# First down projection: each weight block loaded once, the weight sums made on VectorE and moved, the product without token sums put second

## The chip, the cores and the metric

One core of a Trainium2 chip. The time is device microseconds of the core for one execution of the whole program; lower is better. TensorE does the matmuls; VectorE, ScalarE and GpSimd compute beside it; SyncE issues most DMAs (on the hardware queue q1), GpSimd issues those that add to what already lies in the destination (on the software queue q0).

## What is computed

Two feed-forward blocks one after the other on 1024 tokens of width 512. The first ("conditioning") has 1376 hidden features and a low-rank addition of rank 16 per batch entry in each of its three projections; the second has 1792 hidden features and a normalisation before it. All in float32.

```python
def lora_add(base, inp, A, B):
    t = einsum('bri,bni->bnr', A[0][lora_indices], inp)
    return base + einsum('bor,bnr->bno', B[0][lora_indices], t) * 0.5
gate = lora_add(x @ W_gate.T, x, A_gate, B_gate)
up   = lora_add(x @ W_up.T,   x, A_up,   B_up)
act  = silu(gate) * up
down = lora_add(act @ W_down.T, act, A_down, B_down)      # the first down projection
nx   = down * rsqrt(mean(down**2) + 1e-5) * ln_w
out  = x + (silu(nx @ gate_w.T) * (nx @ up_w.T)) @ down_w.T
```

## The kernel before

**Exactness.** Every operand of a matmul is split in two parts of the fast float type: a high part, copied by ScalarE (`hi_...`), and a low part, the raw value minus the high part, from VectorE (`lo_...`). A product is three matmuls (high by high, low by high, high by low).

**Strassen's form.** Each big product is cut in 2x2 blocks and computed as seven products of sums of blocks instead of eight. For that, sums of weight blocks and sums of activation blocks ("token sums", over the two halves of the tokens and of the features) are made first.

**Order of the work.** (1) The first feature tiles; (2) eight groups (`group(j)`, j = 0 to 7, so S1 = 8) of gate and up products of the conditioning block; (3) the first down projection (`c_item`, line 1882), where the change lies; (4) squares, norm and token sums of its result; (5) twelve more groups of gate and up products; (6) the second down projection (line 1990). Each engine has one instruction stream, written out by hand, and semaphores between the streams; nothing is reordered.

**The down projection before.** It has seven products, in the order 11, t2, 21, t3, t4, t1, 22. Each is five items (one per feature tile), an item is two tiles (the two halves of the output features, one PSUM bank each), a tile three matmuls with 512 columns: 30 matmuls a product. "11" and "21" take blocks of `act` as they are; t1 to t4 take token sums, which GpSimd's adding DMAs make in place in `act` (`add_act`), except the fifth tiles of two of them (`last_pair_sums`) and t1's, which VectorE makes. Products 11 and 21 write banks `A_BANK`; t2, t3, t4 write `B_BANK`, and what is in `B_BANK` after t2 must be kept in `wdr` (`keep_u2`, ScalarE) before t3 adds to it; `seed` copies `A_BANK` to `B_BANK` after 11. Before t4's first tile stand `short_c(0, 0)` and `short_c(0, 1)` (line 1896, 12 matmuls of 256 columns), the last short feature tile of 96 rows with the low-rank part; they need both halves of `last_wd`, so VectorE's `lo_w10(1)`.

**Weights before.** The four blocks of the weight come from HBM, 640 KB each. Blocks 11, 12 and 22 are wanted as they are (products 11, 21, t4). The four sums for t2 (11+21+22), t3 (11+21), t1 (21+22) and 22 (11+12+21+22) were made by a plain load and one, two or three adding loads on GpSimd's queue (`add_w`, seven in all), which wait for each other. Where a raw block lies, its low part is written later; the high part lies beside it. The tiles for the weights share memory with work that is over by then, so loads wait for groups (`s_p4`, `s_q2`, `s_p3`).

**Names in the rows.** `down_w_sums_raw` and `down_w_raw` are raw weight blocks; `down_w_sums` and `down_w` their split parts; `xs` the ring of eight split activation items; `last_wd` the short tile's weights; `ws`, `wx` and `wsum` the weights of the gate and up groups with their sums. Group 11 of those (`G1 + 1`, later `G1 + 2` and `G1 + 3`) had its sums made by DMAs too (`two_w`, `more_w`).

## Time and profile before

| | |
|---|---|
| time, median of 3 runs (lowest to highest) | 418.01 us (415.73 to 418.56) |
| the profiled execution, its time | 418.55 us |
| its span, first to last instruction | 416.7 us |
| TensorE busy | 391.0 us (94%) |
| VectorE, ScalarE, GpSimd busy | 328.2, 252.1, 31.3 us |
| granted TensorE clock, mean | 0.975 of full |
| moved by hardware queue q1 / software queue q0 | 33.76 MB in 24.3% / 9.96 MB in 13.5% of the 16 engines' span |

Busy shares are means over the whole span. The first down projection stands between about 127.8 and 210 us. PEclk is the granted clock as a share of 2.4 GHz; 0.50 is 1.2 GHz.

### The profile page before, as it was taken

What the parts mean: (1) busy time and instruction counts of PE and PEld (TensorE: products, weight loads), DVE (VectorE), ACT (ScalarE), POOL (GpSimd) and SP (SyncE); (2) the same over time, 40 slices, a digit from 0 to 9 for tenths busy, and PEclk for the clock granted to TensorE, in tenths of its full rate; (3) what the DMA queues carried; (4) which work ended last, traced back from release to release, by engine and by line L of the source; (5) the groups of instructions that cost most, each with busy time, mean ns of one, the idle gap of its engine ahead of it and who ended that gap; (6) DMA issues with size and microseconds to landing.
All of it is one profiled execution on the core that took longest, in us unless ns stands there. A gap on an engine that the chain in (4) does not pass through costs nothing.

```text
span 416.7 us, 5733 instructions
## 1 busy us (share of the span) xinstructions
PE 391.0 (94%) x1954; PEld 324.3 (78%) x1954; DVE 328.2 (79%) x472; ACT 252.1 (60%) x390; POOL 31.3 (8%) x33
## 2 busy tenths in 40 slices
PE   9999999999999279369989999999999999999997
PEld 6988888888888168268868788888888888888886
DVE  4899987777568187576989988787877869899995
ACT  5879786767573276287565564545555567375730
POOL 6200000000212116010010000000000000000000
PEclk9999999999999779959999999999999999999999
DMA  7630262111699989960340112231313033305112
GB/s 262 186 108 10 78 178 85 50 52 51 200 229 204 289 229 166 251 124 2 88 129 0 51 52 61 83 109 50 102 51 101 22 118 109 130 2 185 56 50 101
DMA packets 18973, 45.90 MB, mean 110 GB/s; under 512 B 2690, under 2 KB 6018, under 8 KB 18946
## 3 DMA queue, kind: packets, MB, share of 16 engines
q1 hardware_dynamic: 13792, 33.76, 24.3%
q0 software_dynamic: 4032, 9.96, 13.5%
q10 hardware_dynamic: 1122, 1.84, 1.3%
q8 instruction: 15, 0.25, 0.2%
q14 instruction: 12, 0.10, 0.1%
HBM read 39.26 MB, written 2.10 MB: 99 GB/s over the span
## 4 chain that ended last, share of the span: by engine, by line
PE 75%; DMA 11%; DVE 6%; ACT 4%; issue 3%; POOL 0%; ACTq 0%; SPq 0%; DVEq 0%; POOLq 0%
PE bank L1627 44%; PE bank L1990 16%; DMA act<-act 7%; DMA down_w_sums_raw<-wc_in 4%; PE bank L1882 4%; PE bank L1845 3%; PE bank L1799 3%; PE bank L1834 3%; PE bank L1637 2%; DVE xs L1088 2%; ACT xs L551 1%; PE bank L1896 1%; PE bank L1793 1%; DVE nx L1356 1%; ACT stack L551 1%
## 5 line engine op out<-in xcount | busy, mean ns | idle before, releaser
L1627 PE MATMUL bank<-xs,ws 128*128 128x512 f32 x840 | 195.9, 390 | 0.9 <-DVE act L1151 0.6
L1627 PEld LDWEIGHTS bank<-xs,ws 128*128 128x128 f32 x840 | 156.3, 188 | 34.2 <-DVE act L1151 1.0
L551 ACT ACTIVATE xs<-act 128x512 fp32r<-128x512 f32 (+1 forms) x73 | 49.9, 702 | 40.6 <-DMA act<-act 15.7
L1088 DVE TENSOR_TENSOR xs<-act,xs 128x512 fp32r<-128x512 f32 (+1 forms) x66 | 49.9, 770 | 4.9 <-ACT xs L551 4.3
L1088 DVE TENSOR_TENSOR ws<-wraw,ws 128x256 fp32r<-128x256 f32 (+2 forms) x45 | 30.1, 671 | 15.9 <-ACT ws L551 15.8
L1882 PE MATMUL bank<-xs,down_w_sums 128*128 128x512 f32 x120 | 29.9, 406 | 10.7 <-ACT bank L551 10.7
L551 ACT ACTIVATE bank<-bank 128x512 f32<-128x512 f32 x34 | 19.3, 576 | 33.9 <-PE bank L1627 33.2
L551 ACT ACTIVATE mu<-bank 128x512 f32<-128x512 f32 x44 | 26.1, 596 | 22.6 <-PE bank L1627 16.0
L1088 DVE TENSOR_TENSOR ws<-wsum,ws 128x1024 fp32r<-128x1024 f32 x20 | 24.5, 1225 | 17.7 <-ACT ws L551 17.7
L1990 PE MATMUL bank<-xs,vs 128*128 128x512 f32 x168 | 38.2, 389 | 0.0
L1990 PEld LDWEIGHTS bank<-xs,vs 128*128 128x128 f32 x168 | 31.5, 188 | 6.5
L1882 PEld LDWEIGHTS bank<-xs,down_w_sums 128*128 128x128 f32 x120 | 23.4, 198 | 15.9 <-issue 10.9
L551 ACT ACTIVATE ws<-wraw 128x256 fp32r<-128x256 f32 (+2 forms) x44 | 26.8, 614 | 7.0 <-PE bank L1627 3.3
L1990 PE MATMUL bank<-xs,ws 128*128 128x512 f32 x120 | 27.7, 389 | 0.0
L1990 PEld LDWEIGHTS bank<-xs,ws 128*128 128x128 f32 x120 | 22.5, 188 | 4.7
L551 ACT ACTIVATE ws<-wsum 128x1024 fp32r<-128x1024 f32 x20 | 21.1, 1053 | 5.8 <-DMA wsum<-wsum 4.0
L551 ACT ACTIVATE stack<-bgu_raw 32x1024 fp32r<-32x1024 f32 (+1 forms) x20 | 22.8, 1138 | 0.3
L1882 PE MATMUL bank<-xs,down_w 128*128 128x512 f32 x90 | 22.7, 408 | 0.0
L623 ACT ACTIVATE act<-bank 128x512 f32<-128x512 f32 (+1 forms) x28 | 16.2, 594 | 8.4 <-PE bank L1637 6.2
L1882 PEld LDWEIGHTS bank<-xs,down_w 128*128 128x128 f32 x90 | 17.8, 201 | 3.7
L1627 PE MATMUL bank<-xs,wx 128*128 128x512 f32 x84 | 19.7, 389 | 0.0
L1627 PEld LDWEIGHTS bank<-xs,wx 128*128 128x128 f32 x84 | 15.8, 188 | 3.3
(146 smaller groups left out, 499.3 us busy)
## 6 DMA issues: line engine op xcount, KB each, us to landing
wraw<-wgu_in SPq DMA_DIRECT2D x22, 512.0 KB, 3.3
down_w_sums_raw<-wc_in POOLq DMA_DIRECT2D x7, 640.0 KB, 9.3
wdr<-vs_in SPq DMA_DIRECT2D x7, 512.0 KB, 3.4
wraw<-vj_in SPq DMA_DIRECT2D x3, 896.0 KB, 4.7
down_w_sums_raw<-wc_in SPq DMA_DIRECT2D x4, 640.0 KB, 5.5
act<-act POOLq DMA_DIRECT2D x4, 512.0 KB, 8.2
down_w_raw<-wc_in SPq DMA_DIRECT2D x3, 640.0 KB, 7.4
wsum<-wbase_in SPq DMA_DIRECT2D x3, 512.0 KB, 7.0
```

What stands on the lines that cost most here:

```text
L551: return nc.scalar.activation(out_ap, in_ap, ACT.Copy, scale=scale)
L623: return nc.scalar.activation(out_ap, in_ap, ACT.Silu, scale=scale)
L1088: return nc.vector.tensor_tensor(out_ap, raw, v32(part), ALU.subtract)
L1356: nc.vector.scalar_tensor_tensor(part, part, lnw[:, h:h + 1], rt[:, 1, :], ALU.mult, ALU.mult).then_inc(s_nx, 1)
L1627: ins = mm(z[:, :], w_slot(j)[:, w, s, k * P:(k + 1) * P], xs[:, c, r, k, :], start=(start and k == 0 and s == 0 and r == 0), stop=(k == 1 ...
L1637: ins = mm(z[0:m, half], stk[c % 2][:, 2 * t + q, cols], t_op[:, half], start=(alone and q == 0), stop=(q == 1), skip_group_check=True)
L1793: mm(B_BANK[i % 2][:, :].rearrange("p (k n) -> p k n", k=KT), one, one.unsqueeze(1).to_broadcast([P, KT, P]), start=True, stop=True)
L1799: mm(UNIT_BANK[i][g][:, cols], w0_tile(s, k, g, i), x_op(k, 0, r)[:, cols], start=(k == 0 and s == 0 and r == 0 and cols.start == 0), stop ...
L1834: mm(UNIT_BANK[n][g][:, :], w0_tile(s, k, g, UNITS[n][0]), x_op(k, 1, r), start=(k == 0 and s == 0 and r == 0), stop=(k == KT - 1 and s == ...
L1845: ins = mm(SHORT_BANK[t][g][:, half], wsh[s][:, k, g, q, :], x_op(k, t, r)[:, half], start=(k == 0 and s == 0 and r == 0 and q == 0), stop ...
L1882: ins = mm(CDOWN[p][1][h][:, :], C_W[p][:, s, k, h * P:(h + 1) * P], slot_c(u, r), start=(p in (C11, CT1) and k == 0 and s == 0 and r == 0 ...
L1990: ins = mm(DOWN[p][3][h][:, :], down_w(i, s)[:, h * P:(h + 1) * P], slot_f(i, r), start=(p < 2 and k == 0 and s == 0 and r == 0), stop=(s ...
```

## The change

(a) Blocks 11, 21, 22 and 12 are loaded once each, without adding, the first of them (11) earlier in SyncE's stream than before, behind `load_stack(4)`. (b) VectorE makes three sums in group 6 (21+22, then 11 added to it, and 11+21) and the fourth (11+12+21+22) in group 7. (c) Two of the four sums lie where a high part will go, so two DMAs from SBUF to SBUF (`move_sum`) bring them to their places; the high parts of products 21 and t2 wait for these moves. (d) Block 22 is loaded again for t4, and t1's weight is a load with one adding load. Seven adding loads of weights become one. (e) The order of the products becomes 11, 21, t2, t3, t4, t1, 22, on all engines. (f) `keep_u2` stands later in ScalarE's stream, behind the high part of t4's weight; TensorE does the first-half tiles of the last two items of t2 first, so that bank 0 can be kept while bank 1 is still added to. (g) The sums of weight group 11 come from VectorE (`sums(G1 + 1)`), not from two DMAs and a load.

```diff
-        CDOWN = (("11", A_BANK), ("t2", B_BANK), ("21", A_BANK), ("t3", B_BANK), ("t4", B_BANK), ("t1", P5_BANK), ("22", P5_BANK))
+        CDOWN = (("11", A_BANK), ("21", A_BANK), ("t2", B_BANK), ("t3", B_BANK), ("t4", B_BANK), ("t1", P5_BANK), ("22", P5_BANK))
...
+            def move_sum(n, to, held):
+                sp.wait_ge(*cw_loaded(n - 2))
+                sp.dma_start(to, held).then_inc(s_cw_ld[n % 2], 16)
...
             load_stack(4)
+            load_down_w(L_11, C_RAW[C11], 0, 0)
             for j in range(7, 11):
                 load_w(j)
             sp.wait_ge(s_ad, 10)
-            load_down_w(C11, 0, 0)
+            load_down_w(L_21, RAW_21, 1, 0)
             sp.wait_ge(s_stklo, 10)
-            load_down_w(CT2, 0, 0)
+            load_down_w(L_22, C_RAW[CT2], 1, 1)
             sp.wait_ge(s_p4, S1 - 2)
-            load_down_w(CT3, 0, 0)
+            load_down_w(L_12, C_RAW[C21], 0, 1)
             load_w(11)
             sp.wait_ge(s_q2, S1)
-            load_down_w(C21, 0, 1)
+            sp.wait_ge(s_csum, SUM_S3)
+            move_sum(M_T3, C_RAW[CT3], RAW_S3)
...
                 sp.dma_start(raw10[0:CR, v, :], w10_in).then_inc(s_w10_ld, 16)
+            sp.wait_ge(s_p4, S1)
+            sp.wait_ge(s_csum, SUM_S4)
+            move_sum(M_22, C_RAW[C22], RAW_S4)
+            sp.wait_ge(s_p3, S1)
+            load_down_w(L_T4, C_RAW[CT4], 1, 1)
...
+            load_down_w(L_T1, C_RAW[CT1], 1, 1)
...
-            pool.wait_ge(*cw_loaded(CT2))
-            add_w(S2_21, CT2, 1, 0)
-            pool.wait_ge(*cw_loaded(CT3))
-            add_w(S3_21, CT3, 1, 0)
-            add_w(S2_22, CT2, 1, 1)
...
-            add_w(S4_21, C22, 1, 0)
-            two_w(G1 + 1)
...
-            add_w(S1_21, CT1, 1, 0)
-            more_w(G1 + 1)
...
-            add_w(S4_22, C22, 1, 1)
...
-            add_w(S4_11, C22, 0, 0)
+            pool.wait_ge(*cw_loaded(L_T1))
+            nc.gpsimd.dma_start(C_RAW[CT1], wc_in[1, 0].rearrange("p (k m) -> p k m", k=KC), accum_op=ALU.add
...
                     lo_w(C11)
+                    sum_w(RAW_S4, C_RAW[CT2], C_RAW[C21], SUM_S4, (L_12,))
...
+                    elif j == S1 - 2:
+                        sum_w(C_RAW[CT2], C_RAW[CT2], RAW_21, SUM_21_22, (L_21, L_22))
+                        sum_w(C_RAW[CT2], C_RAW[CT2], C_RAW[C11], SUM_S2, (L_11,))
+                        sum_w(RAW_S3, RAW_21, C_RAW[C11], SUM_S3)
                     if j != S1 - 1:
                         lo_b(w_of(w_next(j)))
...
+            for u in range(KC * CT2, KC * CT2 + 3):
                 c_item(u)
+            pe.wait_ge(s_clo, KC * CT2 + KC)
+            c_tile(KC * CT2 + 3, 0)
+            c_tile(KC * CT2 + 4, 0).then_inc(s_half, 1)
+            for u in range(KC * CT2 + 3, KC * CT2 + KC):
+                c_tile(u, 1).then_inc(s_cuse, 1)
             pe.wait_ge(s_cw_lo, 4)
+            pe.wait_ge(s_clo, KC * CT3 + 2)
+            pe.wait_ge(s_pc, KEEP_U2 + 1)
+            c_tile(KC * CT3, 0)
+            c_tile(KC * CT3 + 1, 0)
```

**Place 1, VectorE, groups 6 and 7.** Before; `ws<-wsum` is the low part of the sums that TensorE's next G product needs, `act<-mu,bank5` and `act<-mu,bank2` feed the products behind it:

```order
L1088 TENSOR_TENSOR ws<-wraw,ws 128x3x256
L1088 TENSOR_TENSOR ws<-wsum,ws 128x4x256
L1119 TENSOR_TENSOR act<-mu,bank5 128x512
L1148 TENSOR_TENSOR act<-mu,bank2 128x512
L1098 TENSOR_TENSOR wsum<-wraw 128x512
L1101 TENSOR_TENSOR wsum<-wsum,wraw 128x256
L1103 TENSOR_TENSOR wsum<-wsum,wraw 128x256
L1088 TENSOR_TENSOR down_w_11<-down_w_11_raw,down_w_11 128x1280
L1088 TENSOR_TENSOR ws<-wraw,ws 128x3x256
```

Between the splits of group 7's weights (the first two rows) nothing stands. VectorE at the same place now, with the sums at line 1213:

```order
L1074 TENSOR_TENSOR ws<-wraw,ws 128x3x256
L1213 TENSOR_TENSOR down_w_sums_raw<-down_w_sums_raw,down_w_11_raw 128x1280 x2
L1213 TENSOR_TENSOR down_w_sums_raw<-down_w_11_raw 128x1280
L1074 TENSOR_TENSOR ws<-wsum,ws 128x4x256
L1105 TENSOR_TENSOR act<-mu,bank5 128x512
L1134 TENSOR_TENSOR act<-mu,bank2 128x512
L1084 TENSOR_TENSOR wsum<-wraw 128x512
L1087 TENSOR_TENSOR wsum<-wsum,wraw 128x256
L1089 TENSOR_TENSOR wsum<-wsum,wraw 128x256
L1074 TENSOR_TENSOR down_w_11<-down_w_11_raw,down_w_11 128x1280
L1213 TENSOR_TENSOR down_w_sums_raw<-down_w_sums_raw 128x1280
L1074 TENSOR_TENSOR ws<-wraw,ws 128x3x256
```

Three sums of 1280 elements now stand ahead of `ws<-wsum`, and a fourth ahead of the next `ws<-wraw`.

**Place 2, ScalarE, behind product 11.** Before; the first row is the split of the last part of 11, the next those of the weights of t3 and t2, then three parts of t2's token sums; `bank2<-bank0` and `bank4<-bank1` are the seeds that TensorE's second product waits for:

```order
L551 ACTIVATE xs<-act 128x512
L551 ACTIVATE down_w_sums<-down_w_sums_raw 128x1280 x2
L551 ACTIVATE xs<-act 128x512
L551 ACTIVATE xs<-act 128x1024
L551 ACTIVATE xs<-act 128x512
L551 ACTIVATE ws<-wsum 128x4x256
L551 ACTIVATE down_w_12_22<-down_w_12_22_raw 128x1280
L551 ACTIVATE bank2<-bank0 128x512
L551 ACTIVATE bank4<-bank1 128x512
```

Two splits of summed weights and all but the last part of t2 stand ahead of the seeds. ScalarE at the same place now, again from the last part of 11:

```order
L534 ACTIVATE xs<-act 128x512
L534 ACTIVATE down_w_sums<-down_w_sums_raw 128x1280
L534 ACTIVATE xs<-act 128x512
L534 ACTIVATE xs<-act 128x1024 x2
L534 ACTIVATE bank2<-bank0 128x512
L534 ACTIVATE bank4<-bank1 128x512
L534 ACTIVATE down_w_sums<-down_w_sums_raw 128x1280
L534 ACTIVATE xs<-act 128x1024
```

The split of 21's weight stands first, then its three parts (taken from `act` as it is), then the seeds; everything of t2 has moved behind them. The last two rows are the split of t2's weight and t2's first part; behind them stand the low-rank rows of the short tile (four small copies) and a split of `ws<-wsum`.

**Place 3, ScalarE, up to keep_u2 (`wdr<-bank2`, `wdr<-bank4`).** Before, between the seeds and keep_u2:

```order
L551 ACTIVATE act<-bank3 32x128 x4
L551 ACTIVATE xs<-act 128x512
L551 ACTIVATE xs<-act 128x1024
L551 ACTIVATE act<-bank3 32x128 x4
L551 ACTIVATE xs<-act 128x1024
L551 ACTIVATE xs<-act 128x512
L551 ACTIVATE wdr<-bank2 128x512
L551 ACTIVATE wdr<-bank4 128x512
```

Here keep_u2 follows the last parts of t2 and 21 at once. ScalarE now, from t2's second part to keep_u2:

```order
L534 ACTIVATE xs<-act 128x1024
L534 ACTIVATE act<-bank3 32x128 x4
L534 ACTIVATE xs<-act 128x512
L534 ACTIVATE down_w_12_22<-down_w_12_22_raw 128x1280
L534 ACTIVATE xs<-act 128x512 x2
L534 ACTIVATE last_wd<-last_wd_raw 128x4x256
L534 ACTIVATE xs<-act 128x1024
L534 ACTIVATE ws<-wraw 128x3x256
L534 ACTIVATE xs<-act 128x1024
L534 ACTIVATE down_w_12_22<-down_w_12_22_raw 128x1280
L534 ACTIVATE wdr<-bank2 128x512
L534 ACTIVATE wdr<-bank4 128x512
```

`wdr<-bank2`, which TensorE's t3 needs, now has the splits of the weights of t3 and t4, all of t3's parts, half of `last_wd` and a `ws` split ahead of it.

## Rows read from the trace of the kernel before

**Rows 1.** Waits of TensorE between 100 and 260 us: us in total, times, longest.

```profile
PE bank L1882 <- ACT bank L551: 10.7, 1, 10.7
PE bank L1896 <- DVE last_wd L1219: 9.6, 1, 9.6
```

**Rows 2.** The chain that ended last: start us, us, what.

```profile
125.24 9.59 DMA act<-act
...
165.03 12.11 DMA act<-act
```

**Rows 3.** Timeline of TensorE: start us, us, what, count, idle before.

```profile
114.67 5.63 PE L1627 MATMUL bank<-xs,ws 128*128 128x512 f32 x24
...
148.52 8.60 PE L1882 MATMUL bank<-xs,down_w_sums 128*128 128x512 f32 x30 [10.70 <-ACT bank L551]
156.95 6.96 PE L1882 MATMUL bank<-xs,down_w 128*128 128x512 f32 x30
...
180.28 2.93 PE L1896 MATMUL bank<-xs,last_wd 128*128 128x256 f32 x12 [9.57 <-DVE last_wd L1219]
183.01 4.95 PE L1882 MATMUL bank<-xs,down_w 128*128 128x512 f32 x15
...
199.99 1.58 PE L1896 MATMUL bank<-xs,last_wd 128*128 128x256 f32 x12
```

**Rows 4.** Windows of TensorE: us, busy (count), PEclk (granted clock), DMA share, GB/s.

```profile
141.30:141.80 0.50, 0.00 (x0) 0.71 1.07 221
...
175.50:176.00 0.50, 0.00 (x0) 0.64 0.99 397
...
180.20:184.00 3.80, 3.72 (x15) 0.50 0.62 110
```

**Rows 5.** Timeline of VectorE in the last two groups before the down projection.

```profile
113.02 1.23 DVE L1088 TENSOR_TENSOR ws<-wsum,ws 128x1024 fp32r<-128x1024 f32 x1 [4.03 <-ACT ws L551]
...
116.86 0.69 DVE L1098 TENSOR_TENSOR wsum<-wraw 128x512 f32<-128x512 f32 x1
...
118.39 1.49 DVE L1088 TENSOR_TENSOR down_w<-down_w_raw,down_w 128x1280 fp32r<-128x1280 f32 x1
122.88 0.96 DVE L1088 TENSOR_TENSOR ws<-wraw,ws 128x768 fp32r<-128x768 f32 x1 [3.01 <-ACT ws L551]
```

**Rows 6.** Timelines of SyncE's queue and of GpSimd.

```profile
106.29 0.33 SPq L355 DMA_DIRECT2D down_w_raw<-wc_in  x1
106.67 3.85 SPq L355 DMA_DIRECT2D down_w_sums_raw<-wc_in  x2
...
126.11 0.33 SPq L355 DMA_DIRECT2D down_w_raw<-wc_in  x1
129.56 3.17 SPq L411 DMA_DIRECT2D last_wd_raw<-w_in  x4
...
112.01 0.91 POOL L495 DMA_DIRECT2D down_w_sums_raw<-wc_in  x1 [0.43 <-DMA down_w_sums_raw<-wc_in]
```

**Rows 7.** Time to landing: down_w_raw, act additions; both queues, 125 to 140 us.

```profile
DMA to landing us min/median/max: 3.8/7.4/8.0
...
DMA to landing us min/median/max: 6.9/9.6/13.2
...
q0 software_dynamic: 646, 1.69, 61.2%
q1 hardware_dynamic: 785, 1.65, 40.1%
```

**Rows 8.** Timeline of ScalarE in the down projection.

```profile
146.64 1.25 ACT L551 ACTIVATE down_w<-down_w_raw 128x1280 fp32r<-128x1280 f32 x1
147.80 1.06 ACT L551 ACTIVATE bank<-bank 128x512 f32<-128x512 f32 x2
148.88 1.14 ACT L551 ACTIVATE act<-bank 32x128 f32<-32x128 f32 x4
...
161.80 1.05 ACT L551 ACTIVATE xs<-act 128x1024 fp32r<-128x1024 f32 x1
```

More of the change, by code:

```diff
@@ L994, in _ @@
             hi_c(CT3, 2)
-            hi_w(CT4, cw_loaded(CT4))
+            hi_w(CT4, cw_loaded(L_T4))
+            for i in range(2):
+                keep_u2(i)
             hi_b(G1 + 1)
@@ L1478, in _ @@
             lo_c(C11, 2)
[L1479 removed]
             c21(S1 - 1)
[L1481 to L1484 removed]
             lo_w(C21)
[L1486 to L1487 removed]
             for n in range(3):
                 lo_c(C21, n)
[L1490 removed]
+            last_pair_sums()
+            lo_w(CT2)
+            lo_c(CT2, 0)
+            lo_b(G1)
+            lo_c(CT2, 1)
+            lo_c(CT2, 2)
+            sums(G1 + 1)
+            lo_w(CT3)
             lo_short(0)
             lo_c(CT3, 0)
+            lo_w10(0)
             lo_c(CT3, 1)
```

138 lines of the change are left out of this document (62 added, 76 removed).

## The prediction, made before the changed kernel ran

> **What bounds the kernel now.** The page first: TensorE is busy 94% of the span, so only its own waits, a lower clock or less work can change the time; this change takes no matmul away. Next the waits of TensorE [rows 1]: in the stretch of the down projection there are two of size, 10.7 us for a bank copied by ScalarE (the seed ahead of the second product) and 9.6 us for `last_wd` by VectorE (the short tile ahead of t4). Together 20.3 us. The chain that ended last [rows 2] says what stands behind both: adding DMAs of token sums, one of 9.59 us (and a second like it) ahead of the first wait, one of 12.11 us ahead of the second. ScalarE and VectorE are only the last links. The timeline [rows 3] gives the dates: TensorE stops at 148.52 - 10.70 = 137.8 and at 180.28 - 9.57 = 170.7. It also shows what a wait costs afterwards: the product behind the first takes 8.60 us where the next takes 6.96; behind the second, 12 short matmuls take 2.93 us (1.58 later) and 15 long ones 4.95 (half of 6.96 is 3.48). The windows [rows 4] give the reason: the granted clock goes from 1.0 to 0.5 (1.2 GHz) at about 141.5, 3.7 us into the first wait, and at about 175.6, 4.9 us into the second, and is 0.50 from 180.2 to 184. So the full prize is 20.3 + 1.6 + (1.35 + 1.47) = 24.8 us.
>
> **The sums in groups 6 and 7.** VectorE's three sums need blocks 21 and 22. Before, the load issued second landed at 112.0, where GpSimd's wait ends [rows 6]; 21 and 22 are now issued at those two dates, so the first sum starts at 112.0. A sum of 1280 elements has no row; the nearest is the subtraction of the same shape, 1.49 us [rows 5], which I take (above it I see no reason, below it nothing nearer). Three give 116.4. Behind them is queued `ws<-wsum`, 1.23 us, which before ran at 113.02 after an idle of 4.03 us [rows 5]: now 117.7. TensorE's G product of group 7 wants it at 117.5 (24 matmuls from 114.67 in 5.63 us [rows 3], six of P7 and six of Q1 ahead of the six of G), so this costs 0.3 us. The fourth sum falls into the 3.01 us that VectorE waited ahead of 122.88 [rows 5]: 0.3 us again, the same 0.3. If that cover were gone, each sum would cost 1.49. The early load of 11 stands ahead of a weight load of SyncE that is used two groups later, so it costs nothing; without that cover, its landing time, 3.8 us [rows 7].
>
> **First wait (place 2).** t2's token sums leave the path; product 21 takes blocks of `act` that are ready. What is late next is its weight: the high part waits for the move of 11+21, issued when the q2 of group 7 is done, as the load at 126.11 was [rows 6], now 126.4. Behind the landing stand 1.25 (ScalarE) [rows 8] + 1.49 + 0.69 (VectorE) [rows 5], 3.5 us with the hand-overs; the seeds (1.06 us [rows 8]) run beside the low-rank matmuls that follow product 11, and TensorE arrives at 137.8 + 0.3 = 138.1. So the move may take 8.2 us. A DMA from SBUF to SBUF that doesn't add has no row. Its bounds are the 640 KB loads, 3.8 to 8.0 us, and the additions within `act`, 6.9 to 13.2 [rows 7]; I take 6, below the loads' median since fewer additions run beside it. The wait is then zero; at 9.6 it would be 1.4, at 13.2 it would be 5.0. Product 21 runs 138.1 to 145.1.
>
> **t2's weight.** It waits for the second move (11+12+21+22), since that sum lies where t2's high part goes. SyncE issues it behind four loads that take it 3.17 us from 129.56 [rows 6]: 133.1. Its landing, X, sets everything behind. From 125 to 140 us the two queues filled the 16 engines: q1 moved 1.65 MB in 40.1% of 15 us, 3.65 us a MB; q0 1.69 MB in 61.2%, 5.4 us a MB [rows 7]. From 126.4 on, q1 has the two moves and the four loads, 0.655 + 0.79 + 0.655 = 2.1 MB, 7.7 us; q0 has additions of 1.3 MB beside it, 7.0 us. Together 14.7: X = 141.1, a landing time of 8. Ends: 3.8 gives 136.9, 13.2 gives 146.3. Then 1.25 + 1.49 + 1.23 puts t2's first items at 145.1, just when TensorE is there; t2 runs to 152.1. The DMA page of the Trainium skill ("DMA: Bandwidth & Descriptors", section "Anatomy of one DMA") has a fit, for the software queue, of about 2 us plus the bytes over 436 GB/s, for 640 KB 3.5 us, an estimate by that page; the first load's 3.8 [rows 7] agrees with it, the crowded ones don't. By that rule the sum would end at the low rival below.
>
> **keep_u2 (place 3).** t3's first tile waits for it. From X, ScalarE has in a row two weight splits beside t2's own, parts, low-rank copies, a `last_wd` half. At 1.16 from start to start for 1280 elements, 1.08 for two of 512, 1.14 for four small ones, 0.95 for 1024 [rows 8], three of 1280, six of 1024, four of 512 (keep_u2 itself with them), one of 768 (0.8) and two sets of small ones make 14.4 us: 155.5. TensorE is ready at 152.1: a new wait of 3.4 us, with t3 to 162.4.
>
> **Second wait.** The short tile still waits for `lo_w10(1)`, and its place behind all of t4's parts on VectorE hasn't changed. t2's last part is done on VectorE at X + 7.5 (ScalarE's 6.8 to its high part, 0.69). Then VectorE has no idle time: the new sums of group 11 1.55 (116.86 to 118.39, [rows 5]), two weight splits 2.8, nine of 1024 elements 10.2, four of 512 2.4, one of 768 0.9, each 0.1 under its duration as on ScalarE: 17.9. So it ends at X + 25.4 = 166.5 where it ended at 180.24. TensorE waits 166.5 - 162.4 = 4.1 us instead of 9.57. t4's token sums, issued from 137 on, land by 150 to 158 (9.6 each, two in a row), and VectorE asks for the last at 163; at 13.2 each they would cost 0.3. The adding load for t1 is issued near 150 and wanted at 161. The two DMAs and the load for group 11 go: they covered nothing on the path.
>
> **The sum.** 180.3 - 166.5 = 13.8 us. Behind that point all streams keep their order and start aligned as before, so the rest follows at the same distance. The 2.8 us of low clock go if the clock holds through the 4.1 us wait; it fell 3.7 and 4.9 us into the two waits [rows 4], so I take half, 1.2. 418.55 - 13.8 - 1.2 = 403.5 for the profiled execution. The median of the runs is 0.5 below that one: **403.0**.
>
> **The rivals.** (1) X near 137: the moves land like a lone load. For it: the first load's 3.8 us [rows 7]; against it, that both queues together filled the engines from 125 to 140 us. VectorE then sets the end itself at about 163 (it can't begin t2 before its pair sums, 138.1 + 1.4; then 23.3 us of work): 17.3 + 2.8, 398 to 400. This is also where the page's fit leads. Chance 0.17. (2) X of 144 to 148, q1 held up by additions (13.2 was seen): each us costs one, and the clock falls again: 407 to 411. Chance 0.2. (3) The sums hold group 6: block 22 takes the 8.0 us of the slowest load [rows 7], lands at 114.7, and the G product waits 3 us, with more behind it if the fourth sum is late too; the rest keeps its gain: 406 to 409. Chance 0.06. (4) Slower than before: moves within SBUF run at a fraction of a load's speed. Place: the landing of the second. Price: one for one. It decides from X = 180.3 - 25.4 = 154.9, a move of 22 us, against 13.2 for the slowest row; at 25 us the time is 421. Chance 0.03. (5) The change does not do what it says, in that the wait only changes its name: keep_u2 and VectorE's stream together give back 7.5 of the 20.3 already in my sum; that they give back all would need ScalarE and VectorE to be 13 us later than their rows add up to. 415 to 418. Chance 0.04. My forecast, X of 139 to 143, 400.5 to 406.5, has the remaining 0.5.
>
> **How the numbers follow.** The range from 398 to 410 takes in the forecast, rival 1, rival 3 and most of rival 2, leaving out about 0.1 to 0.15; its ends are X = 137 with the clock held and X = 146.3 (13.2 us) with it lost. A change within 1% (4.2 us), about what a measurement of this kernel can tell, is rival 5 and a part of rival 2: 0.05. Slower by over 1%: 0.03. Faster: 0.92.
>
> **What would show it.** In the profile after: no wait of TensorE over 1.5 us near 138 (first step right); a wait of TensorE on ScalarE's `wdr` near 152 of 2 to 5 us; a wait for `last_wd` of 3 to 5 us ending near 166; the landing of the second move near 141 by ScalarE's idle time ahead of `down_w_sums`; VectorE's three sums of 1.49 us from 112.0. I'd be wrong if the moves take under 5 or over 11 us, if group 7's G product waits over 1 us, or if ScalarE or VectorE waits in the chain behind X for a DMA that I took as landed.

## The result and the profile after

The changed kernel takes 404.13 us (median of 4 runs, 401.47 to 404.83) where the kernel before takes 416.87 us beside it (414.08 to 418.56): a ratio of 0.9689, 95% interval 0.9616 to 0.9763. The forecast was 403.0. The profiled execution took 404.83 us with a span of 402.0 us, against 416.7; the granted clock rose from 0.975 to 0.992. The executions of one kernel differ among themselves: the four of the changed kernel have spans from 399.8 to 402.4 us, and the six of a later comparison (after_again, below) from 399.8 to 402.6. The traces here show one execution each, so differences of one or two microseconds between two traces are weaker evidence than the dates within one.

The page of the kernel after, first the busy times, then the queues, then the chain that ended last:

```profile
PE 391.0 (97%) x1954; PEld 324.0 (81%) x1954; DVE 334.7 (83%) x478; ACT 252.8 (63%) x389; POOL 23.8 (6%) x25
...
q1 hardware_dynamic: 13792, 33.89, 25.1%
q0 software_dynamic: 2752, 5.37, 7.7%
...
PE 80%; DVE 10%; issue 4%; ACT 3%; DMA 2%; SPq 1%; DVEq 0%; ACTq 0%
```

The chain of the kernel before:

```profile
PE 75%; DMA 11%; DVE 6%; ACT 4%; issue 3%; POOL 0%; ACTq 0%; SPq 0%; DVEq 0%; POOLq 0%
```

TensorE's busy time is the same to a tenth of a microsecond, so the net change is in its waiting. That is a balance, not a standstill: the product behind the old first wait is 1.6 us shorter, t3 1.7 us longer. The software queue moves about half of what it did. In the chain, DMA has fallen from 11% to 2% of the span: the adding DMAs of [rows 2] are out of it.

Waits of TensorE between 100 and 260 us, the two of size (they answer to [rows 1]):

```profile
PE bank L1885 <- ACT wdr L534: 3.4, 1, 3.4
PE bank L1899 <- DVE last_wd L1216: 2.2, 1, 2.2
```

20.3 us of waiting have become 5.6. Neither row is what is left of an old wait in its old place: the first stands two products later than the old first one. The timeline of TensorE shows the dates (for [rows 3]):

```profile
115.34 5.65 PE L1630 MATMUL bank<-xs,ws 128*128 128x512 f32 x24
...
138.43 13.94 PE L1885 MATMUL bank<-xs,down_w_sums 128*128 128x512 f32 x60
155.78 8.70 PE L1885 MATMUL bank<-xs,down_w 128*128 128x512 f32 x30 [3.41 <-ACT wdr L534]
166.68 2.66 PE L1899 MATMUL bank<-xs,last_wd 128*128 128x256 f32 x12 [2.20 <-DVE last_wd L1216]
169.13 4.23 PE L1885 MATMUL bank<-xs,down_w 128*128 128x512 f32 x15
```

The row of 60 matmuls is products 21 and t2 in one piece, at twice 6.97 us and without a wait ahead: the old first wait is gone. The 24 matmuls of group 7 that had to wait for VectorE's sums, if anything did, take 5.65 us against 5.63. They also start 0.67 us later than in [rows 3]; such a shift is there from the first stretch of the trace (38 matmuls in 9.46 us instead of 8.77), and from 56 us on order_only, which has no sums in group 6, has it too. So it is not the price of those sums. The short tile starts at 166.68 instead of 180.28, 13.6 us earlier.

What stands behind the two waits is in the chain that ended last (start us, us, what):

```profile
130.24 0.34 SPq L411
...
134.34 6.45 DMA down_w_sums_raw<-down_w_sums_raw
```

SyncE issues the four loads of line 411, then the second move (`move_sum` for t2's weight), which lands at 134.34 + 6.45 = 140.8. From there the chain runs through ScalarE's and VectorE's splits, of which the last is the second half of `last_wd` (`lo_w10(1)`, 165.49). ScalarE's timeline shows both landings as the ends of its idle time (for [rows 8]):

```profile
132.50 1.28 ACT L534 ACTIVATE down_w_sums<-down_w_sums_raw 128x1280 fp32r<-128x1280 f32 x1 [3.14 <-DMA down_w_raw<-down_w_sums_raw]
...
140.82 1.28 ACT L534 ACTIVATE down_w_sums<-down_w_sums_raw 128x1280 fp32r<-128x1280 f32 x1 [2.66 <-DMA down_w_sums_raw<-down_w_sums_raw]
...
155.04 1.09 ACT L534 ACTIVATE wdr<-bank 128x512 f32<-128x512 f32 x2
```

From the second row on ScalarE has no idle time up to `wdr<-bank` (keep_u2), for which t3 waits. VectorE's timeline, first in groups 6 and 7 (for [rows 5]), then at the end of its stream for the short tile:

```profile
112.19 3.09 DVE L1213 TENSOR_TENSOR down_w_sums_raw<-down_w_sums_raw,down_w_raw 128x1280 f32<-128x1280 f32 x2 [2.53 <-DMA down_w_sums_raw<-wc_in]
...
116.60 1.22 DVE L1074 TENSOR_TENSOR ws<-wsum,ws 128x1024 fp32r<-128x1024 f32 x1
...
165.40 1.22 DVE L1216 SCALAR_TENSOR_TENSOR last_wd<-last_wd_raw,last_wd 128x1024 fp32r<-128x1024 f32 x1
```

Two sums in the first row, the third at 115.20 with 1.49 us, the first as block 22 lands, and the split that group 7 wants is done at 117.82.

The windows of TensorE over the two waits (us, busy (count), granted clock, DMA share, GB/s; for [rows 4]):

```profile
155.50:156.00 0.50, 0.22 (x1) 1.00 0.05 10
156.00:158.00 2.00, 2.00 (x7) 0.70 0.00 0
...
165.50:166.60 1.10, 0.00 (x0) 1.00 0.87 148
166.60:168.00 1.40, 1.32 (x7) 0.65 0.69 132
168.00:169.00 1.00, 1.00 (x7) 0.50 0.00 0
```

In this trace the clock is 1.00 (2.4 GHz) throughout each wait and falls to 0.50 (1.2 GHz) only when TensorE is at work again, about 1 us after the first wait and under half a microsecond after the second. That is why t3 takes 8.70 us, not 6.96. (In other traces it falls within the wait; see short_first.)

### The profile page after: what moved, and what is told of

Read it like the earlier page. It is cut to its first block, busy times and chain, and to the rows that moved or that the text cites. A ratio compares the mean times of both kernels' runs of the same rounds, so it can differ in the third digit from the quotient of the medians.

```text
span 402.0 us, 5731 instructions
## 1 busy us (share of the span) xinstructions
PE 391.0 (97%) x1954; PEld 324.0 (81%) x1954; DVE 334.7 (83%) x478; ACT 252.8 (63%) x389; POOL 23.8 (6%) x25
## 4 chain that ended last, share of the span: by engine, by line
PE 80%; DVE 10%; issue 4%; ACT 3%; DMA 2%; SPq 1%; DVEq 0%; ACTq 0%
PE bank L1630 49%; PE bank L2004 16%; DVE xs L1074 3%; PE bank L1802 3%; PE bank L1848 3%; PE bank L1837 3%; PE bank L1640 2%; ACT xs L534 2%; DMA down_w_sums_raw<-down_w_sums_raw 2%; PE bank L1885 1%; SPq L411 1%; PE bank L1796 1%; PE bank L1899 1%; DVE act L1236 1%; PE bank L1743 1%
## 5 line engine op out<-in xcount | busy, mean ns | idle before, releaser
L1885 PE MATMUL bank<-xs,down_w_sums 128*128 128x512 f32 x120 | 28.3, 391 | 0.0
L1885 PE MATMUL bank<-xs,down_w 128*128 128x512 f32 x90 | 23.7, 421 | 3.4 <-ACT wdr L534 3.4
L1885 PEld LDWEIGHTS bank<-xs,down_w_sums 128*128 128x128 f32 x120 | 22.3, 188 | 4.7 <-issue 0.2
```

What stands on the lines that cost most here:

```text
L1885: ins = mm(CDOWN[p][1][h][:, :], C_W[p][:, s, k, h * P:(h + 1) * P], slot_c(u, r), start=(p in (C11, CT1) and k == 0 and s == 0 and r == 0 ...
```

## The experiments

Three theories were put to the chip. **The prediction's theory**: the gain is the first wait, gone because the second product no longer needs token sums, and the second wait, cut down to what hangs on the second move's landing, one for one, through VectorE's stream; keep_u2 is beside that path. **A first rival, the order alone**: the order of the products does it all, and the sums on VectorE and their moves buy nothing. **A second rival, the queue alone**: the sums do it all, by keeping weight additions out of GpSimd's queue. Theories on single terms (the clock, keep_u2, the cover of the sums) are told with their runs.

All ratios are against the kernel before on the same chip; its median was 417.09 us for the first four rows, 416.34 for the next four, 416.49 for the last four (11 runs each). Waits are those of TensorE in the down projection.

| run | median us | ratio (95%) | span | clock | waits, us |
|---|---|---|---|---|---|
| order_only | 403.34 | 0.9728 (0.9652 to 0.9803) | 400.4 | 0.996 | seed 0.4, keep_u2 1.4, short tile 3.8 |
| sums_only | 408.71 | 0.9817 (0.9755 to 0.988) | 406.9 | 0.983 | seed 3.6, short tile 5.4 |
| move_first | 401.72 | 0.9626 (0.9571 to 0.9681) | 400.8 | 0.991 | keep_u2 1.1, short tile 3.6 |
| short_first | 400.53 | 0.9614 (0.9566 to 0.9662) | 399.5 | 0.991 | keep_u2 3.5 |
| after_again | 402.58 | 0.9677 (0.964 to 0.9715) | 402.4 | 0.992 | keep_u2 3.4, short tile 2.2 |
| keep_early | 403.58 | 0.9691 (0.9655 to 0.9728) | 401.9 | 0.992 | t3's parts 3.0, short tile 2.7 |
| one_sum_twice | 403.64 | 0.97 (0.9665 to 0.9735) | 402.0 | 0.992 | group 7 1.6, keep_u2 3.4, short tile 1.1 |
| combined | 399.86 | 0.9616 (0.9582 to 0.965) | 398.0 | 0.995 | copy_u3 3.1 |
| old_gpsimd_order | 410.35 | 0.9868 (0.9804 to 0.9932) | 408.2 | 0.983 | seed 0.4, keep_u2 1.4, short tile 11.1 |
| order_only_again | 402.65 | 0.9683 (0.9636 to 0.973) | 399.5 | 0.996 | seed 0.3, keep_u2 1.3, short tile 3.8 |
| waits_filled | 401.99 | 0.966 (0.9613 to 0.9706) | 400.3 | 1.000 | keep_u2 0.2, short tile 0.3 |
| combined_2 | 402.04 | 0.967 (0.9621 to 0.9718) | 399.4 | 0.996 | t4's parts 2.1 |

### Which part carries the gain: order_only, sums_only

**order_only** has the products, the streams of ScalarE and TensorE and keep_u2's place as in the changed kernel, but makes the weight sums as before, by plain loads and adding loads on GpSimd's queue; group 11's sums stay on VectorE. On that queue the token sums of t4 stand ahead of the weight additions for 22 and t1.

```diff
-                        sum_w(RAW_S3, RAW_21, C_RAW[C11], SUM_S3)
...
+            add_w(S2_21, CT2, 1, 0)
+            add_w(S3_21, CT3, 1, 0)
+            add_w(S2_22, CT2, 1, 1)
...
             add_act(T4_01, act_c(KC, KC + 2, 0), act_c(0, 2, 0))
             add_act(T4_23, act_c(KC + 2, KC + 4, 0), act_c(2, 4, 0))
+            add_w(S4_21, C22, 1, 0)
```

> The new kernel with its order of products and VectorE's sums of group 11, but with the weight sums made by seven adding DMAs and no moves, as before; GpSimd issues t4's token sums ahead of the weight additions that aren't due yet. Theory (both waits came from adding DMAs that TensorE met too early; the order takes the first away whoever makes the sums): no wait near 138, the short tile starts within 1 us of the new kernel's 166.7, and 1 to 4 us are lost later, where the high parts of t1 and 22 wait for chained additions: 405 to 408 us. Rival (the gain comes from taking the weight sums off GpSimd's queue): half of it or more is lost, 411 us or over.

Measured: 403.34 us in the first comparison, whose interval is wide (one of its four executions took 408.21 us), and in a second one with more rounds (order_only_again, below) 402.65, 0.9683. The timeline of TensorE:

```profile
138.84 7.07 PE L1879 MATMUL bank<-xs,down_w 128*128 128x512 f32 x30 [0.37 <-ACT bank L545]
...
154.06 7.04 PE L1879 MATMUL bank<-xs,down_w_sums 128*128 128x512 f32 x30 [1.36 <-ACT wdr L545]
164.95 2.10 PE L1893 MATMUL bank<-xs,last_wd 128*128 128x256 f32 x12 [3.85 <-DVE last_wd L1215]
```

The first wait is as good as gone, and the short tile starts 1.7 us earlier than after the whole change: without the moves nothing hangs on their landing. The expected loss of 1 to 4 us behind it did not come. The last wait is now one for a token sum of t4, seen on ScalarE:

```profile
159.54 0.63 ACT L545 ACTIVATE xs<-act 128x512 fp32r<-128x512 f32 x1 [2.01 <-DMA act<-act]
```

**sums_only** keeps the old order (11, t2, 21) and keep_u2's old place behind the parts of 21, with the sums on VectorE, the moves and the short GpSimd queue of the change. One thing more differs from the changed kernel: the second move, which t2's weight needs first here, is issued ahead of the four loads, as in move_first below.

```diff
-        CDOWN = (("11", A_BANK), ("21", A_BANK), ("t2", B_BANK), ("t3", B_BANK), ...
+        CDOWN = (("11", A_BANK), ("t2", B_BANK), ("21", A_BANK), ("t3", B_BANK), ...
...
+            move_sum(M_22, C_RAW[C22], RAW_S4)
             sp.wait_ge(s_c22f, S1 // 2)
             sp.wait_ge(s_c12f, S1 // 2)
             for v in range(4):
                 sp.dma_start(raw10[0:CR, v, :], w10_in).then_inc(s_w10_ld, 16)
...
-            move_sum(M_22, C_RAW[C22], RAW_S4)
```

> The new kernel's loads, VectorE's sums and moves, but the products in the old order 11, t2, 21, with keep_u2 in its old place and the second move ahead of the four loads. Theory: t2's weight lands at about 139, TensorE waits 3.5 to 4.5 us near 138, product 21's parts and with them t4's token sums come later, and the short tile starts near 170.5: 407 to 409 us. Rival (the order counts for little once the weight sums are off GpSimd's queue): 405 us or less.

Measured: 408.71 us. TensorE, and ScalarE ahead of the seeds (`bank<-bank`):

```profile
142.27 16.46 PE L1883 MATMUL bank<-xs,down_w_sums 128*128 128x512 f32 x60 [3.57 <-ACT bank L535]
...
171.29 2.93 PE L1897 MATMUL bank<-xs,last_wd 128*128 128x256 f32 x12 [5.38 <-DVE last_wd L1214]
```

```profile
138.39 1.27 ACT L535 ACTIVATE down_w_sums<-down_w_sums_raw 128x1280 fp32r<-128x1280 f32 x1 [8.82 <-DMA down_w_sums_raw<-down_w_sums_raw]
139.56 2.08 ACT L535 ACTIVATE xs<-act 128x512 fp32r<-128x512 f32 x3
141.55 1.06 ACT L535 ACTIVATE bank<-bank 128x512 f32<-128x512 f32 x2
```

The first wait falls from 10.7 to 3.6 us without any change of the order. The token sums of t2 were there when ScalarE came to them (no idle time ahead of its three parts); it waited for the moved weight, and the seeds stood behind. So the second rival is right that the queue alone takes most of the first wait, and wrong that it takes all. The move's place helps here: in the changed kernel it lands at 140.8, 2.4 us later, which would leave a first wait of about 6 us, an estimate from these two dates. What the order is worth is therefore read against move_first, which issues the move at the same place and ran in the same comparison: 408.71 against 401.72, 7.0 us, and 6.1 us in the spans. The end of the 60 matmuls accounts for it: 3.8 us later start (142.27 against 138.45), 2.5 us more for the low clock (16.46 us against 13.94). Against the changed kernel itself the difference is 4.6 us, because there the later move takes a part back.

### What order_only shares with the change: old_gpsimd_order, order_only_again

order_only differs from the kernel before in two things that could matter, the order of the products and that of GpSimd's DMAs (group 11's sums and keep_u2's place, which it also has from the change, were not tried by themselves). To part the two, **old_gpsimd_order** puts the weight additions back between and ahead of the token sums on GpSimd's queue, as before, in the new order of the products.

```diff
+            pool.wait_ge(*cw_loaded(L_22))
+            add_w(S4_21, C22, 1, 0)
             pool.wait_ge(s_clo, KC * C21 + 2)
             add_act(T4_01, act_c(KC, KC + 2, 0), act_c(0, 2, 0))
+            pool.wait_ge(*cw_loaded(L_T1))
+            add_w(S1_21, CT1, 1, 0)
             pool.wait_ge(s_clo, KC * C21 + 4)
             add_act(T4_23, act_c(KC + 2, KC + 4, 0), act_c(2, 4, 0))
```

> As order_only (new order of products, all weight sums by adding DMAs), but GpSimd issues them in the order of the kernel before: t4's token sums stand behind weight additions that wait for loads. Theory (what the fewer adding DMAs buy is an unblocked GpSimd queue for token sums, which order_only had got by its own order of issue): t4's last token sum lands near 168 or later instead of 159, the short tile starts at 170 or later, 4 to 8 us over order_only. Rival (the queue's order is free, the order of products does it all): within 1 us of order_only.

Measured: 410.35 us. The first wait stays away (the second product starts at 138.83), and the second is back in full (11.1 us). The timeline of TensorE, then the chain that ended last:

```profile
172.23 2.93 PE L1893 MATMUL bank<-xs,last_wd 128*128 128x256 f32 x12 [11.12 <-DVE last_wd L1215]
```

```profile
147.13 9.35 DMA act<-act
...
157.13 11.97 DMA act<-act
```

The first of t4's token sums is issued at 147.13, behind a weight addition for which GpSimd had waited 11.15 us; in order_only it went out at 139.69. The last lands at 169.1 instead of 159.5; in the kernel's code it waits for the first one's landing. GpSimd issues in the order of its stream: a token sum whose operands are ready stands behind an addition whose load is not. That costs 172.23 - 164.95 = 7.3 us at the short tile, and 7.7 us in the medians of the same comparison (410.35 against 402.65).

> The order_only kernel once more with five rounds, to be set beside the new kernel's five. Theory after the first run (VectorE's sums and the moves buy nothing over adding DMAs once the order is changed and GpSimd's queue is free): within 1 us of the new kernel's ratio of 0.968. Rival: 1.5 us or more slower than it.

Measured: 402.65 us, 0.9683, against 0.9677 for the changed kernel with as many rounds (below). The first rival is right in this sense: with the products in the new order and token sums first on GpSimd's queue, sums on VectorE and moves bring nothing more that these runs can tell; the intervals would hide a difference of up to about 2 us. Each of the two waits has its own remedy, the order for the first and the queue for the second, and the change as made holds both.

### The second move's landing: move_first

**move_first** issues the second move ahead of the four loads of line 411.

```diff
+            sp.wait_ge(s_p4, S1)
+            sp.wait_ge(s_csum, SUM_S4)
+            move_sum(M_22, C_RAW[C22], RAW_S4)
             for v in range(4):
                 sp.dma_start(raw10[0:CR, v, :], w10_in).then_inc(s_w10_ld, 16)
-            sp.wait_ge(s_p4, S1)
-            sp.wait_ge(s_csum, SUM_S4)
-            move_sum(M_22, C_RAW[C22], RAW_S4)
```

> The second move is issued ahead of the four loads of the short tile's weights, nothing else. Theory (everything up to the short tile hangs on its landing, one for one): landing 1.5 to 2.5 us earlier, the short tile 1.3 to 2.3 us earlier, time 1.5 to 2 us under the new kernel's. Rival (TensorE or the pair sums set that time): under 0.5 us.

Measured: 401.72 us, 0.9626. The move is issued at 133.00 instead of 134.34. TensorE:

```profile
153.47 7.04 PE L1885 MATMUL bank<-xs,down_w 128*128 128x512 f32 x30 [1.09 <-ACT wdr L534]
164.14 2.93 PE L1899 MATMUL bank<-xs,last_wd 128*128 128x256 f32 x12 [3.62 <-DVE last_wd L1216]
166.87 5.22 PE L1885 MATMUL bank<-xs,down_w 128*128 128x512 f32 x15
```

ScalarE begins the split of t2's weight at 138.26 instead of 140.82, 2.56 us earlier, and the short tile starts 2.54 us earlier: one for one, as the prediction's theory has it. Landing took 5.2 us here. But the span of the traced execution, 400.8 us, is only 1.2 to 1.6 us shorter than those of the changed kernel's two traces. The low clock now falls on the tiles behind the short one (2.93 + 5.22 us against 2.66 + 4.23) and takes 1.3 us back. In the changed kernel the same low clock hit t3 first, where a wait hid it. The six executions show how much such an accident is worth: three with a mean clock of 0.991 have spans of 400.5 to 400.9 us, one with 0.996 has 399.2, and two with 1.000 have 396.9 and 397.2. The same kernel, with the same stream, can keep the clock or lose it.

### Who holds the second wait: short_first, keep_early

**short_first** moves the second half of `last_wd` ahead of t4's parts, on ScalarE and on VectorE.

```diff
+            lo_w10(1)
             for n in range(3):
                 t1(n)
                 lo_c(CT4, n)
-            lo_w10(1)
```

> The second half of the short tile's weights is split ahead of t4's parts on ScalarE and VectorE, nothing else. Theory (VectorE's stream, with the short tile's weights last in it, holds TensorE there): the 2.2 us wait goes and with it the low clock behind it, 3 to 4 us under the new kernel. Rival (t4's parts are as late, so the wait only moves behind the short tile): under 1 us.

Measured: 400.53 us, 0.9614. TensorE:

```profile
155.79 9.95 PE L1885 MATMUL bank<-xs,down_w 128*128 128x512 f32 x30 [3.49 <-ACT wdr L534]
165.58 1.59 PE L1899 MATMUL bank<-xs,last_wd 128*128 128x256 f32 x12
```

The second wait is gone; the span is 2.5 us shorter than that of the changed kernel (2.9 against after_again), a little less than was expected, since t3 lost more to the clock (9.95 us instead of 8.70). The window over the end of its wait:

```profile
155.00:156.00 1.00, 0.21 (x1) 0.55 0.01 0
```

The clock had fallen at about 155.1, before TensorE went on at 155.79, and came back near 161.9. Up to there nothing differs from the changed kernel, the start of t3 and the wait agree to 0.1 us, and still the fall came 1.7 us earlier and the low stretch was longer. VectorE's order held the second wait, as predicted.

**keep_early** moves keep_u2 ahead of two weight splits and a part of t3 on ScalarE.

```diff
+            for i in range(2):
+                keep_u2(i)
             hi_a(G1 + 1)
             hi_c(CT3, 2)
             hi_w(CT4, cw_loaded(L_T4))
-            for i in range(2):
-                keep_u2(i)
```

> keep_u2 stands behind t3's second part on ScalarE, nothing else. Theory (VectorE's chain sets the end of the stretch, keep_u2 only stands beside it): t3 starts at most 0.6 us earlier, since VectorE's part for its second and third item ends at 155.2, the short tile at the same 166.7 within 0.2, time the same within 0.5 us. Rival (keep_u2's wait is a loss of its own): 2 to 3.4 us faster.

Measured: 403.58 us, 0.9691, beside 402.58 and 0.9677 for **after_again**, the changed kernel in the same comparison.

> The new kernel once more, as the base of the runs beside it: 404 us within 1, waits of 3.4 and 2.2 us.

TensorE in keep_early:

```profile
155.43 8.67 PE L1885 MATMUL bank<-xs,down_w 128*128 128x512 f32 x30 [2.96 <-DVE xs L1074]
166.80 2.93 PE L1899 MATMUL bank<-xs,last_wd 128*128 128x256 f32 x12 [2.70 <-DVE last_wd L1216]
```

t3 now waits for its own low parts from VectorE and starts 0.68 us earlier than in after_again (156.11); the short tile starts within 0.2 us of where it did there (167.01). The medians, 1.0 us apart, lie within the scatter. The wait for keep_u2, the longest one in the profile after, was worth nothing by itself: two streams arrive at t3 within a microsecond of each other, and both lie ahead of a later wait that VectorE sets anyway.

### The cover of VectorE's sums: one_sum_twice

One of the three sums in group 6 is made a second time.

```diff
                         sum_w(RAW_S3, RAW_21, C_RAW[C11], SUM_S3)
+                        v.wait_ge(s_csum, SUM_S3 - 1)
+                        nc.vector.tensor_tensor(RAW_S3, RAW_21, C_RAW[C11], ALU.add).then_inc(s_csum, 1)
```

> The third weight sum (11+21) is made twice in a row on VectorE in group 6; nothing else. Theory: the three sums just fill VectorE's slack there, so one more costs TensorE 1.0 to 1.4 us at the G product of group 7, and all behind it as much. Rival (there is slack left, as the missing wait in the profile says): under 0.3 us.

Measured: 403.64 us, 0.97, against 402.58 and 0.9677 for after_again: the intervals can tell neither the expected 1.0 to 1.4 us nor nothing. TensorE:

```profile
119.57 3.02 PE L1632 MATMUL bank<-xs,ws 128*128 128x512 f32 x12 [1.55 <-DVE ws L1074]
...
157.34 9.83 PE L1887 MATMUL bank<-xs,down_w 128*128 128x512 f32 x30 [3.37 <-ACT wdr L534]
168.23 1.70 PE L1901 MATMUL bank<-xs,last_wd 128*128 128x256 f32 x12 [1.06 <-DVE last_wd L1216]
```

1.49 us more on VectorE makes 1.55 us of wait in group 7: the three sums of the change use up all the cover there is, and not a fourth more. (In after_again the 24 matmuls there took 5.95 us instead of 5.63, so the three sums themselves cost 0.3 us in that execution.) The place and price were as expected; whether everything behind comes as much later stays open. Up to t3 it does (157.34 against 156.11). In this trace the clock then gives it back: it falls at about 156.4, still within the wait, t3 takes 9.83 us, and it has returned before the short tile (1.70 us against 2.89, and 3.59 for the 15 behind it against 3.97).

### What the low clock costs: waits_filled

15 and 16 matmuls of a constant (line 1894) are added where TensorE would wait for keep_u2 and for the short tile's weights, into a bank that is overwritten afterwards. `copy_u3` waits for them as well.

```diff
+            pe.wait_ge(s_c12, S1)
+            fill(15)
             pe.wait_ge(s_cw_lo, 4)
             pe.wait_ge(s_clo, KC * CT3 + 2)
...
+            fill(16)
             pe.wait_ge(s_w10lo, 2)
```

> The new kernel with 15 and 16 extra matmuls of 512 columns, on constants, into a bank that is free, put where TensorE waits for keep_u2 and for the short tile; their results are overwritten. Theory (TensorE's clock falls because of the waits, also of one of 3.4 us, and costs 1.8 us behind the second): granted clock 1.0 from 150 to 175, t3 in 7.0 us instead of 8.7, the short tile at the same 166.7, then 1.6 to 2.0 us less: about 2 us faster. Rival (the low clock is hidden by the stretch behind it): under 0.5 us.

Measured: 401.99 us, 0.966, with a granted clock of 1.000 over the span. The timeline of TensorE:

```profile
155.62 7.07 PE L1887 MATMUL bank<-xs,down_w 128*128 128x512 f32 x30 [0.21 <-ACT wdr L535]
...
166.50 1.70 PE L1907 MATMUL bank<-xs,last_wd 128*128 128x256 f32 x12 [0.30 <-DVE last_wd L1218]
168.04 3.59 PE L1887 MATMUL bank<-xs,down_w 128*128 128x512 f32 x15
```

t3 starts when it did and ends 1.8 us sooner; the short tile starts within 0.2 us of where it did (VectorE sets it), and it and the 15 behind it take 1.6 us less. The span is 1.7 to 2.1 us shorter than that of the two profiles of the changed kernel. So the low clock behind the two short waits cost the traced executions about 1.8 us, nearly all of it behind the second. The medians don't confirm it as a mean gain: 401.99 against 402.58 us, 0.966 against 0.9677. All six executions with filled waits have spans of 399.8 to 400.5 us, as short as the shortest of the changed kernel (399.8 to 402.6), and none is long; what made the short ones of the changed kernel short, at clocks of 0.991 to 0.996, no trace shows.

### The best version: combined, combined_2

**combined** takes move_first and lets everything that does not need the weight of t4 go ahead of it: t3's parts, both halves of `last_wd`, then t4's.

```diff
             lo_w(CT3)
             lo_c(CT3, 0)
             lo_c(CT3, 1)
+            sums(G1 + 1)
+            lo_c(CT3, 2)
+            lo_short(0)
+            lo_w10(0)
+            lo_a(G1 + 1)
+            lo_w10(1)
+            lo_w(CT4)
```

> Second move first; on ScalarE and VectorE t3's parts and keep_u2 ahead of the short tile's and group 11's work, and the second half of the short tile's weights ahead of t4's. Theory: no wait of TensorE between 138 and 159, the short tile at 159.5 to 160.5, clock at full, a wait under 1 us inside t4; 396 to 398 us. Rival (the wait moves to t4's parts or to the stretch of squares and norm behind, which has its own chain of VectorE and ScalarE): 399 us or more.

Measured: 399.86 us, 0.9616, the lowest median of the study, though short_first (0.9614) and move_first (0.9626) can't be told from it; its runs (399.41 to 400.65) lie below all those of the changed kernel. TensorE, then ScalarE:

```profile
152.10 6.96 PE L1889 MATMUL bank<-xs,down_w 128*128 128x512 f32 x30
158.97 1.70 PE L1903 MATMUL bank<-xs,last_wd 128*128 128x256 f32 x12
163.77 5.26 PE L1889 MATMUL bank<-xs,down_w 128*128 128x512 f32 x15 [3.11 <-ACT bank L534]
```

```profile
163.10 1.05 ACT L534 ACTIVATE bank<-bank 128x512 f32<-128x512 f32 x2
```

Both waits are gone and a third, of 3.1 us, has come: t4 waits for `copy_u3` (`bank<-bank`), which stands on ScalarE behind the split of t1's weight (1.25 us from 161.94). The short tile came even earlier than expected, at 158.97, but the time is above the expected 396 to 398 us and where the rival had it: the wait had moved.

**combined_2** puts `copy_u3` ahead of that split, and group 11's low part behind t4's parts.

```diff
             for n in range(2):
                 hi_c(CT4, n)
-            hi_b(G1 + 1)
+            for i in range(2):
+                copy_u3(i)
             hi_c(CT4, 2)
             hi_c(CT1, 0)
+            hi_b(G1 + 1)
             hi_w(CT1, (s_cw_add, 16))
-            for i in range(2):
-                copy_u3(i)
```

> The combined kernel with the copy of bank B to D (copy_u3) and group 11's low part moved: the copy ahead of t4's last part, group 11's split behind t4's parts on both engines. Theory: the wait of 3.1 us on the copy shrinks to the 1 us that t4's first part takes on VectorE, the first half of t4 ends 2 to 3 us earlier, 2 us faster than combined. Rival (VectorE's stream up to the squares sets the end whatever stands first): within 0.7 us of combined.

Measured: 402.04 us, 0.967. TensorE, t4's first half, and the last wait for the squares' copy at the end of the norm:

```profile
161.75 1.63 PE L1889 MATMUL bank<-xs,down_w 128*128 128x512 f32 x6 [1.54 <-DVE xs L1075]
...
194.58 0.49 PE L1910 MATMUL bank<-xs,ones 128*128 128x512 f32 x1 [1.39 <-ACT xs L818]
```

The 3.1 us wait became 2.1 us of waits for VectorE (1.54 in the first row, 0.55 ahead of the rest of that half), t1 starts 2.4 us earlier than in combined (171.34 against 173.73), and the end of the norm is no earlier (combined has the last row at 194.44, with a wait of 0.92). ScalarE and VectorE, who make the squares, set the pace there, and TensorE's lead is spent in front of them. That shows why nothing is gained. Why the traced execution is slower by 1.4 us stands right behind, in the first matmuls after the norm (combined, then combined_2):

```profile
196.74 3.00 PE L1634 MATMUL bank<-xs,ws 128*128 128x512 f32 x12 [0.31 <-DVE xs L1075]
```

```profile
195.71 5.44 PE L1634 MATMUL bank<-xs,ws 128*128 128x512 f32 x15
```

Combined has three such matmuls ahead of its row (0.86 us from 195.57) and ends the fifteen at about 199.7, combined_2 at about 201.1. The granted clock is 1.00 throughout in combined; in combined_2 it falls at about 196.2, behind the wait of 1.39 us and a short one, and is 0.50 from 197 to 198. From there on the two traces stay 1.4 us apart (198 to 200 us at 0.60 is the last of it), which is the difference of the spans. It isn't the whole of the medians' 2.2 us: one execution of combined_2 had a clock of 1.000 and a span of 399.6, no shorter. The rest stays open.

## Why the prediction was right

**What bounds.** It said that adding DMAs stand behind both waits. Shown: the chain has lost them, and old_gpsimd_order brings the second wait back with two of them in its chain (9.35 and 11.97 us).

**The sums in groups 6 and 7.** Predicted from 112.0, with `ws<-wsum` done at 117.7 and 0.3 us lost. Measured 112.19 and 117.82, and nothing lost in this trace, since TensorE came 0.67 us later by the trace's shift; in after_again, where the sums began at 112.59, 0.3 us were. That the cover was just used up is shown by one_sum_twice.

**First wait.** Predicted zero, with 8.2 us of room for the first move; it took 5.6 (6 was taken). Shown by its absence. What the prediction did not say is that the shorter queue, with the second move issued early, does two thirds of this without the new order (sums_only).

**The second move.** Predicted issue at 133.1, landing in 8 us, X = 141.1. Measured 134.34 and 6.45 us, X = 140.8. Two errors cancel: the four loads ahead occupied SyncE 4.00 us from 130.24 instead of 3.17 from 129.56, and the move was faster than the sum over both queues had it. The moves took 5.6 and 6.5 us beside additions and loads. The fit that the Trainium skill gives for the software queue ("DMA: Bandwidth & Descriptors", "Anatomy of one DMA"), an estimate of 3.5 us for such a size, was low for both, which went over the hardware queue; by it the first rival would have come in.

**keep_u2.** Predicted a wait of 3.4 us ended at 155.5; measured 3.41, ended at 155.78. The date was right to 0.3 us; counted from the measured landing, 15.0 us went by where the rows had added up to 14.4. That this wait lies beside the path is shown by keep_early.

**Second wait.** VectorE's stream was predicted to end at X + 25.4 = 166.5; measured 166.62, which is 25.8 us behind the measured X. The wait was predicted at 4.1 us, with 3 to 5 named as the sign, and was 2.2. The mis-sized term is t3's end, "with t3 to 162.4", which is t3 at full clock: it ran at half the clock for a part, took 8.70 us and ended at 164.5. That didn't move the short tile. The slope of one for one from the landing of the second move is shown at the short tile by move_first, and that `lo_w10(1)` at the end of VectorE's stream is the holder by short_first.

**The clock.** The prediction had the clock held through the new waits with an even chance, and took "half" of 2.8 us as 1.2; half is 1.4 (and its full prize of 24.8 us adds up to 24.7). These slips are small beside what follows. In the traced execution it did not hold; it fell behind both waits. Behind the second, 2.66 + 4.23 us against the 2.93 + 4.95 of [rows 3] gives 1.0 us. The right number came by a wrong picture, so in part by luck: the low clock was taken as the price of a long wait, and it followed waits of 2.2 and 3.4 us; waits_filled puts what it still cost the traced executions at 1.8 us.

**The sum.** 13.6 + 1.0 us in the trace where 13.8 + 1.2 was predicted; the spans differ by 14.7. The times differ by less, 12.7 us in the medians, which is within the interval of the ratio (the predicted 403.0/418.01 = 0.964 lies in it). Of the profiled executions, the time outside of the span was 2.8 us after and 1.85 before, which none of the prediction's steps covers; and the one before lies 1.7 us above its median, the one after 0.7.

**The rivals.** The low one needed a landing near 137; it came at 140.8. The one on the other side, moves within SBUF at a fraction of a load's speed, is refuted by 5.6 and 6.5 us for 640 KB. (A "part of rival 2" can't be within 1% of the kernel before, since that rival ends at 411; its 0.01 changes nothing.) That the wait only changes its name is right for 3.4 us of 20.3.

**What the prediction missed** is a question that it didn't ask: which part of the change earns the gain. The four sums on VectorE and the two moves, on which most of its working was spent, equal the old adding loads within what the runs can tell (0.9677 and 0.9683), provided these stand behind the token sums.

## What to carry to other kernels

When one engine issues two kinds of DMA in the order of its stream, look first at whether one that is ready stands behind one whose operand is still to come: putting the token sums ahead was worth 7.3 us here and needs no other engine. To place a wait, add up each engine's own rows from the last DMA that it waits for; that was right to 0.4 us over 25 us and to 0.6 over 15, and it tells that the longest wait in a profile (3.4 us for keep_u2) can be worth nothing while the next (2.2 us) is worth 2.5. Gains of one or two microseconds at such a place are not read from the date of one instruction, since the clock after a short wait may take back half of them: compare the ends of the stretch, and the spans and clocks of several executions, since one kernel's own can lie 4 us apart (move_first).

## What the runs showed of the hardware

**The clock falls after short waits too, and at no fixed point.** In the stretch of the down projection, the rows behind waits of 1.36, 1.09 and 0.37 us are at full speed (7.04, 7.04 and 7.07 us for 30 matmuls), those behind 2.96 to 3.49 us are not (8.67 to 9.95 us), and 2.20 us were enough to make the short tile slow (2.66 us against 1.58). Behind the norm, 1.39 us and a short wait were followed by a fall in combined_2. In the changed kernel the fall came when TensorE was at work again, 1.0 and 0.3 us after the waits, so a window over the wait itself shows 1.00 and hides it; in short_first and one_sum_twice it came within the wait, 0.7 and 0.9 us before its end. In the kernel before, with waits of 10 us, it came within the wait [rows 4]. Putting matmuls of no use into the waits kept the clock at 1.000 in all six executions.

**What the fall costs is not fixed by the schedule.** The same wait of 3.4 to 3.5 us, ended at the same 155.8, made t3 take 8.70 us in the changed kernel and 9.95 in short_first; 1.2 us later, in one_sum_twice, it was 9.83, and there the clock was back before the short tile. move_first lost it in some executions and kept it in others, 400.8 us against 397.

**Moves within SBUF.** A plain DMA from SBUF to SBUF of 640 KB on the hardware queue took 5.6 and 6.5 us beside other traffic, and 5.2 us where it was issued ahead of the loads (move_first and sums_only). Adding DMAs within `act` took 9.35 us for 512 KB and 11.97 us for 256 KB in old_gpsimd_order, so beside other traffic the size did not set the time.
